# Gathering experts' rows as 16 dense tiles and copying each use within SBUF, in a two-layer mixture-of-experts and attention kernel

## Chip, cores and metric

The kernel runs on one core of a Trainium2 chip. The metric is the device time of one execution, in microseconds; before the change the median of three runs is 521.12 us (520.67 to 521.65).

## What is computed

The input x has 4 x 256 = 1024 tokens of width 256. Three blocks follow one another, each on a layer norm of x: half of a feed-forward layer is added, then attention with 16 heads of width 128, then half of the same feed-forward layer again. The feed-forward layer is what the change touches:

```python
shared = silu(g) * u @ shared_down_w.T            # g, u: 704 wide
shared = sigmoid(x @ shared_gate_w.T) * shared
probs  = softmax(x @ gate_w.T)                    # 8 experts
top_w, top_i = top_k(probs, 2); top_w /= top_w.sum()
he  = silu(x @ w1[e, :176].T) * (x @ w1[e, 176:].T)
out = sum over the 2 chosen e of top_w * (he @ w2[e].T) + shared
```

Each token goes to 2 of 8 experts, so there are 2048 pairs of token and expert.

## The kernel before

**Tiling.** Tokens are handled in NT = 8 blocks of 128. A pair gets a slot: the experts' pairs stand one after the other, and each expert's start is padded to a multiple of 128. With 2048 pairs and eight experts at most NM = 16 + 7 = 23 tiles of 128 slots are needed, each of one expert. The kernel always works through 23.

**Routing.** `route` (L731) picks the two experts, `ranks` (L1119) counts on TensorE, `slots` (L769) makes slot numbers. `rows_of_slots` (L813) writes one-hot rows (`row_hot`), `tiles_of_slots` (L800) one-hot tiles times a token number (`token_hot`, 23 columns for each of two parts). `slot_tokens` (L1131) multiplies the two in 16 small bf16 matmuls, so that for each slot its token stands in PSUM; it comes behind `shared_up(7)` in PE's order (L1163). `tokens` (L834) turns this into `place` (where a row is written back) and `tok_i` (where it is read), in four linked VectorE instructions. "Linked" means that each waits for the one before by a semaphore. `tile_experts` (L821) finds each tile's expert in three more.

**Expert tiles.** For tile m, POOL gathers 128 rows of the normed x from DRAM (`gather`, L567) into one of XR = 10 buffers; PE turns it (`tile_in`, L1140), ACT and DVE split it in a high and a low part (`tile_high` L630, `tile_low` L856), PE multiplies (`up` L1179), ACT and DVE make silu times product, PE turns this (`inner_turn` L1190) and multiplies again (`down` L1196), ACT copies the result out of PSUM (`tile_out` L686) into one of YR = 6 buffers, and POOL scatters it to DRAM (`scatter`, L575). `step` (L1211) is PE's order for three tiles in flight.

**Order on the queues.** The order on every engine is written out by hand. POOL issues gathers and scatters in one queue:

```python
for m in range(NM + OUT_LAG):        # L581, OUT_LAG = 12
    if m < NM: gather(m)
    if m >= OUT_LAG: scatter(m - OUT_LAG)
```

PE comes to the tiles from the shared expert: `first_down(1)`, then `shared_up(latest, first_tile)` (L1226, latest = 8), whose middle holds `first_tile` with `tile_in(0)`; then PE waits for `s_hl` 8, the low part of shared chunk 7 (`shared_low(7)`, L756, on DVE), ahead of `tile_in(1)` (L1227). The DVE order there is L911 to L928: `shared_mul(6)`, `tokens`, `tile_experts`, `shared_low(6)`, `gate_weights`, `lows_of("experts")`, `shared_mul(7)`, `shared_low(7)`, `shared_out(0)`, `tile_low(0)`. The weights are also split in high and low parts, in 23 jobs (`job_low`, L430) shared between POOL and DVE by the tables at L51 to L54; jobs 19 to 22 are DVE's `lows_of("experts")` in layer one.

**The end of a layer.** SP waits until all scatters have landed (L537), loads both rows of every token from DRAM (L539), and DVE adds them to x (`add`, L965, L975). In layer two the results then go out (L546).

Of the kernel before, what the change touches and what calls it, by code (L numbers as in the profile page):

```python
# [5 lines left out]
FP32 = mybir.dt.float32  # L6
FP32R = mybir.dt.float32r
BF16 = mybir.dt.bfloat16
# [5 lines left out]
P = 128  # L14
# [3 lines left out]
KD = D // P  # L18
# [11 lines left out]
STW = 3 * D  # L30
# [4 lines left out]
NM = TOP_K * NT + NE - 1  # L35
# [4 lines left out]
OUT_LAG = 12  # L40
XR = 10
YR = 6
NST = 4
# [11 lines left out]
HIGHS_FIRST = {"turn0": (1, 2), "logits0": (3, 4, 5), "silu0": (6,), "high0": (7,), "turn1": (8,), "silu2": (9, 10),  # L55
               "logits1": (11, 12), "silu3": (13, 14), "silu5": (15,), "high5": (16, 17, 18), "silu6": (19,),
               "silu7": (20, 21, 22)}
# [8 lines left out]
C_M128 = C_DESC + NE  # L66
C_LT = C_M128 + NT
# [4 lines left out]
C_VOID = C_J + TOP_K * NT  # L72
# [8 lines left out]
def constants():  # L81
# [10 lines left out]
    c[:, C_M128:C_M128 + NT] = P * np.arange(NT)  # L92
# [5 lines left out]
    c[:, C_J:C_J + TOP_K * NT] = VOID + np.arange(TOP_K * NT)  # L98
    c[:, C_VOID:C_VOID + NM] = P * np.arange(NM) + r[:, None]
# [4 lines left out]
def macaron(nc, x_in, consts, wgate, wgu, wd, w1, w2, wqkv, wo, bqkv, bo, out):  # L104
    ctx = ExitStack()
    with ctx:
# [15 lines left out]
        xn = sbuf("xn", [P, NT, D])  # L122
# [25 lines left out]
        s_xe = [sem(f"s_xe{b}") for b in range(XR)]  # L148
# [9 lines left out]
        area = sbuf("area", [P, NST * STW])  # L158
        assert QKV + (XR + YR - NT - 2) * D <= NST * STW and QKV + 2 * TOK + 2 * D <= 2 * NE * D
# [112 lines left out]
        def ffn(tag, first, n, after):  # L272
# [7 lines left out]
            with loc:  # L280
# [8 lines left out]
                tile_hot = bank[5][:, P:P + TOP_K * NT * NM].rearrange("p (a b) -> p a b", b=NM)  # L289
# [5 lines left out]
                spare = [area[:, QKV + (2 + b) * D:QKV + (3 + b) * D] for b in range(XR + YR - NT - len(lgT))]  # L295
                xe = [xn[:, b, :] for b in range(NT)] + spare[:XR - NT]
                ye = lgT + spare[XR - NT:]
                assert len(xe) == XR and len(ye) == YR
# [5 lines left out]
                token_hot = sb("token_hot", [P, TOP_K * NT, 2, NM], BF16)  # L304
                place = sb("place", [P, NM], I32)
                tok_i = sb("tok_i", [P, NM], I32)
                he = [sb(f"he{b}", [P, IM]) for b in range(2)]
# [15 lines left out]
                best = sb("best", [P, NT])  # L323
                best2 = sb("best2", [P, NT])
                lead = sb("lead", [P, NT])
# [3 lines left out]
                tiles_of = in_bank(at_tiles, [NE])  # L329
                base = sb("base", [P, NE])  # L330
# [53 lines left out]
                def ring_uses(m, depth):  # L384

                    return (0 if first else -(-(NM - m % depth) // depth)) + m // depth
# [1491 lines left out]
```

## Time and profile before

| | |
|---|---|
| median of three runs | 521.12 us |
| the profiled execution, its own time | 521.58 us |
| its span in the profile | 519.8 us |
| PE busy | 503.7 us, 97% |
| DVE busy | 348.1 us, 67% |
| POOL busy | 279.2 us, 54% |
| ACT busy | 276.0 us, 53% |
| granted TensorE clock, mean | 0.996 |

"Layer one" below is the first feed-forward layer, about 0 to 112 us of the span, "layer two" the second, about 400 to 520 us; attention lies between. The span is the time between the first and last instruction that the profile shows; the run's own time is 1.8 us longer. Rows of the timeline give the start in microseconds from the span's start, the duration, the engine, the line, what is written from what, the count, and in brackets how long the engine had been idle and what ended that.

### The profile page before, as it was taken

How to read it: one execution, taken by the hardware profiler on the slowest of the kernel's cores; microseconds unless marked ns; L12 is line 12 of the kernel's file. 1: busy time of each engine (PE TensorE's matmuls, PEld its weight loads, DVE VectorE, ACT ScalarE, POOL GpSimd, SP SyncE). 2: the span in 40 equal slices, each digit the busy share in tenths (PEclk: the TensorE clock that was granted, in tenths of full speed). 3: DMA queues.
4: the chain of work that ended last, by engine and by line, in shares of the span. 5: the costliest groups of instructions: out<-in, count | busy, mean ns of one | idle time of the engine just before them, and what ended most of it. 6: DMA issues, size and time to landing. Idle time of an engine off the chain costs nothing.

```text
span 519.8 us, 10686 instructions
## 1 busy us (share of the span) xinstructions
PE 503.7 (97%) x3329; PEld 452.5 (87%) x3329; DVE 348.1 (67%) x922; ACT 276.0 (53%) x815; POOL 279.2 (54%) x371
## 2 busy tenths in 40 slices
PE   8999999998999999999999999999999999999994
PEld 4787999887798998999988989999988788899983
DVE  5788766489464775856846847658558578866646
ACT  3983666624462654645636736546445465466540
POOL 1896777732861671652734716716542242677740
PEclk9999999999999999999999999999999999999998
DMA  8951333252002001010010010010001230233335
GB/s 274 388 191 52 105 106 106 103 164 70 21 0 62 2 22 61 20 61 0 20 61 0 20 61 15 14 52 20 0 2 42 81 123 0 83 102 106 108 123 193
DMA packets 20128, 39.41 MB, mean 76 GB/s; under 512 B 2944, under 2 KB 10496, under 8 KB 20096
## 3 DMA queue, kind: packets, MB, share of 16 engines
q1 hardware_dynamic: 15680, 26.92, 15.6%
q0 software_dynamic: 4416, 12.06, 7.1%
q8 instruction: 20, 0.33, 0.3%
q14 instruction: 12, 0.10, 0.1%
HBM read 29.80 MB, written 9.18 MB: 75 GB/s over the span
## 4 chain that ended last, share of the span: by engine, by line
PE 88%; DVE 7%; DMA 1%; issue 1%; POOL 1%; ACT 1%; SPq 0%; POOLq 0%; DVEq 0%
PE bank L183 21%; PE bank L185 20%; PE bank L184 20%; PE bank L1708 5%; PE bank L1720 4%; PE bank L1707 3%; PE bank L1749 3%; PE bank L1144 2%; DVE x_res L975 2%; PE bank L1020 2%; PE bank L189 1%; PE bank L1747 1%; PE bank L190 1%; DMA xn<-y_by_token 1%; PE bank L1192 1%
## 5 line engine op out<-in xcount | busy, mean ns | idle before, releaser
L1452 POOL TENSOR_TENSOR s_a<-s_a,rr_a 128x128 f32<-128x128 f32 x64 | 25.7, 401 | 133.6 <-DVE rr_a L1569 132.8
L1502 ACT ACTIVATE s_a<-s_a,mn_a 128x128 f32<-128x128 f32 (+1 forms) x128 | 57.1, 458 | 18.6 <-DVE mn_a L1563 18.4
L183 PE MATMUL bank<-xT_h,area_h 128*128 128x512 f32 x124 | 51.3, 414 | 0.0
L1495 ACT ACTIVATE qk_a<-bank,bias_a 128x512 f32<-128x512 f32 x32 | 22.0, 688 | 51.2 <-PE bank L185 48.5
L185 PE MATMUL bank<-xT_h,area_l 128*128 128x512 f32 x124 | 48.6, 392 | 0.0
L184 PE MATMUL bank<-xT_l,area_h 128*128 128x512 f32 x124 | 48.5, 391 | 0.0
L571 POOL DMA_INDIRECT xn<-x_normed,tok_i_f x38 | 37.2, 979 | 20.1 <-issue 9.8
L1517 ACT ACTIVATE area_h<-bank,bias_a 128x256 fp32r<-128x256 f32 x64 | 29.0, 478 | 29.3 <-PE bank L1749 28.6
L1551 DVE TENSOR_SCALAR qk_a<-bank,bias_a 128x512 f32<-128x512 f32 x32 | 24.0, 750 | 29.9 <-PE bank L185 29.9
L1563 DVE TENSOR_REDUCE mn_a<-s_a 128x1 f32<-128x128 f32 (+1 forms) x128 | 39.2, 347 | 2.2
L1559 DVE SCALAR_TENSOR_TENSOR s_a<-bank,cst 128x384 f32<-128x384 f32 x64 | 35.2, 549 | 8.1 <-PE bank L1708 8.0
L183 PE MATMUL bank<-area_h,xT_h 128*128 128x256 f32 x128 | 40.3, 315 | 0.0
L1454 POOL TENSOR_TENSOR s_a<-s_a,rr_a 128x256 f32<-128x256 f32 x64 | 39.3, 614 | 0.0
L183 PE MATMUL bank<-area_h 128*128 128x256 f32 x128 | 38.6, 301 | 0.0
L1708 PE MATMUL bank<-qk_a 128*128 128x256 f32 x128 | 38.2, 381 | 0.0
L577 POOL DMA_INDIRECT y_by_token<-rows_f,place_f x32 | 31.4, 982 | 9.7 <-issue 7.6
L185 PE MATMUL bank<-area_h,area_l 128*128 128x256 f32 x128 | 36.2, 283 | 0.0
L184 PE MATMUL bank<-area_l,area_h 128*128 128x256 f32 x128 | 36.2, 282 | 0.0
L185 PE MATMUL bank<-area_h,xT_l 128*128 128x256 f32 x128 | 36.1, 282 | 0.0
L184 PE MATMUL bank<-area_l,xT_h 128*128 128x256 f32 x128 | 36.1, 282 | 0.0
L1580 DVE SCALAR_TENSOR_TENSOR area_l<-bank,bias_a,area_h 128x256 fp32r<-128x256 f32 x64 | 30.1, 479 | 8.4 <-ACT area_h L1517 7.8
L183 PE MATMUL bank<-xT_h,wgu_h 128*128 128x512 f32 x88 | 35.4, 402 | 0.0
(210 smaller groups left out, 1712.1 us busy)
## 6 DMA issues: line engine op xcount, KB each, us to landing
area<-in_wqkv SPq DMA_DIRECT2D x8, 768.0 KB, 4.2
area_r<-in_w SPq DMA_DIRECT2D x16, 256.0 KB, 4.3
w_r<-in_w SPq DMA_DIRECT2D x8, 352.0 KB, 7.4
x_normed<-xn SPq DMA_DIRECT2D x4, 512.0 KB, 4.9
area<-in_wo SPq DMA_DIRECT2D x8, 256.0 KB, 2.6
xn<-y_by_token SPq DMA_DIRECT2D x8, 256.0 KB, 4.0
x_res<-in_x_in SPq DMA_DIRECT2D x4, 256.0 KB, 4.4
wgu_r<-in_wgu SPq DMA_DIRECT2D x4, 256.0 KB, 7.0
```

The lines of the kernel that those rows point to most:

```text
L183: pe.matmul(psum, lhs[0], rhs[0], start=first, stop=False)
L184: pe.matmul(psum, lhs[0], rhs[1], start=False, stop=False)
L185: return pe.matmul(psum, lhs[1], rhs[0], start=False, stop=last)
L571: pool.indirect_dma_start(xe[m % XR], None, xd, bass.IndirectOffsetOnAxis(ap=tok_i[:, m:m + 1], axis=0)).then_inc(s_xe[m % XR], 16)
L577: pool.indirect_dma_start(yd, bass.IndirectOffsetOnAxis(ap=place[:, m:m + 1], axis=0), ye[m % YR], None).then_inc(s_yst[m % YR], 16)
L1454: pool.tensor_tensor(s[b][:, P:3 * P], s[b][:, P:3 * P], rr[:, b, 1:2].to_broadcast([P, 2 * P]), ALU.mult).then_inc(s_p, 1)
L1502: act.activation(s[b][:, cols], s[b][:, cols], ACT.Exp, bias=mn[:, b, t:t + 1], scale=-1.0, accum_out=rs[:, b, t:t + 1]).then_inc(s_e, 1)
L1517: act.activation(zT_h[:, h, bt * SEQ:(bt + 1) * SEQ], bank[ZB[u % 2]][:, 0:SEQ], ACT.Identity, bias=bias[:, 2, h:h + 1]).then_inc(s_zh, 1)
L1559: dve.scalar_tensor_tensor(s[b][:, :], bank[3 + u % 2][:, 0:3 * P], -INV_SCALE, cst[:, C_MASK:C_MASK + 3 * P], ALU.mult, ALU.max).then_inc ...
L1563: dve.tensor_reduce(mn[:, b, t:t + 1], s[b][:, cols], op=ALU.min, axis=AX.X).then_inc(s_mn, 1)
L1580: dve.scalar_tensor_tensor(zT_l[:, h, cols], bank[ZB[u % 2]][:, 0:SEQ], bias[:, 2, h:h + 1], zT_h[:, h, cols].bitcast(FP32), ALU.add, ALU. ...
L1708: pe.matmul(b[:, P:3 * P], q[:, t0 + P:t0 + 2 * P], k[:, t0:t0 + 2 * P], start=True, stop=True).then_inc(s_sc, 1)
```

## The change

The 2048 pairs are laid out with no padding, as NX = 16 dense tiles. A dense tile can hold rows of more than one expert. There are still 23 uses ("items"): one for each tile and expert that meet, and one more for unused ones. POOL gathers only the 16 dense tiles, into XR = 12 buffers. For each item but the first SP reads from `tile_x` which buffer holds its tile and copies it within SBUF (128 KB) into one of XI = 4 buffers `xi`, from which PE turns it; item 0 is turned straight from buffer 0. Rows of a tile that belong to another expert get a place in a void part of DRAM. Copy m waits for gather m (m below 16; gathers of buffers 8 and 9 share a semaphore, as do 10 and 11) and for `tile_in(m - 4)`. Gathers 12 to 15 wait for copies 7 to 10. The result buffers fall from 6 to 4.

POOL issues gathers 0 to 3, in layer one then the low parts of weight jobs 20 to 22, then gathers 4 to 11, then scatters 0 to 3, then gathers 12 to 15 by turns with scatters 4 to 6, then the other scatters. Job 19 goes to POOL too, ahead of the gathers; ACT makes the high parts of jobs 19 to 22 behind `shared_silu(6)`.

On DVE `slots` has two linked instructions fewer, `tokens` is one instruction, `items_of_experts` adds six small ones ahead of it, and `tile_experts` has ten in place of three. `items_of_slots` adds three and a second set of one-hots 23 columns wide; `places` has three and waits for a second set of 16 matmuls on PE, `item_tokens`. `slot_tokens` becomes 32 matmuls of 16 columns, and moves to the middle of `shared_up(7)`. The norms are as they were. The core of the diff:

```diff
+NX = TOP_K * NT
+NM = NX + NE - 1
...
-XR = 10
-YR = 6
-NST = 4
+XR = 12
+YR = 4
+XI = 4
...
-POOL_FIRST = {"rstd0": (2,), "normed": (3, 5, 6, 7, 8, 9, 10, 11, 12, 13, 14, 15, 16, 17, 18)}
+POOL_FIRST = {"rstd0": (2,), "normed": (3, 5, 6, 7, 8, 9, 10, 11, 12, 13, 14, 15, 16, 17, 18, 19), "gathers": (20, 21, 22)}
...
-LOWS_FIRST = {"stats1": (1,), "xn1": (4,), "experts": (19, 20, 21, 22)}
+LOWS_FIRST = {"stats1": (1,), "xn1": (4,)}
...
+                    x_at = sp.alloc_register(f"x_at_{tag}")
+                    sp.wait_ge(s_expert, 2)
+                    for m in range(1, NM):
+                        sp.reg_load(x_at, tile_x[0:1, m:m + 1])
+                        if m == 1:
+                            sp.wait_ge(s_xe[0], 16 * (ring_uses(0, XR, NX) + 1))
+                        if m < NX:
+                            sp.wait_ge(s_xe[gathered(m)], (32 if m % XR >= NT else 16) * (ring_uses(m, XR, NX) + 1))
+                        if m > XI:
+                            sp.wait_ge(s_tx, m - XI + 1)
+                        sp.dma_start(xi[:, m % XI, :], xe[:, sp.snap(x_at, min_val=0, max_val=XR - 1), :]
+                                     ).then_inc(s_xi[m % XI], 16)
...
-                    def gather(m):
-                        if m >= XR:
-                            pool.wait_ge(s_tx, m - XR + 1)
+                    def gather(t):
+                        if t >= XR:
+                            m = t - XR + NE - 1
+                            pool.wait_ge(s_xi[m % XI], 16 * (copies_before(m) + 1))
+                            pool.wait_ge(s_tx, 1)
                         pool.indirect_dma_start(
-                            xe[m % XR], None, xd,
-                            bass.IndirectOffsetOnAxis(ap=tok_i[:, m:m + 1], axis=0)).then_inc(s_xe[m % XR], 16)
+                            xe[:, t % XR, :], None, xd,
+                            bass.IndirectOffsetOnAxis(ap=tok_i[:, t:t + 1], axis=0)).then_inc(s_xe[gathered(t)], 16)
...
-                    for m in range(NM + OUT_LAG):
-                        if m < NM:
-                            gather(m)
-                        if m >= OUT_LAG:
-                            scatter(m - OUT_LAG)
+                    for t in range(XR):
+                        gather(t)
+                        if t == 3:
+                            lows_of("gathers")
+                    pool.wait_ge(s_tok, 2)
+                    for m in range(NM):
+                        scatter(m)
+                        if XR <= XR + m - 3 < NX:
+                            gather(XR + m - 3)
...
+                    def hot(tile, into, n, blocks):
+                        copies = [P, TOP_K * NT, n]
+                        part = tile_hot[:, 0:TOP_K * NT * n].rearrange("p (a b) -> p a b", b=n)
+                        link(dve.tensor_tensor(part, tile[:, :].unsqueeze(2).to_broadcast(copies),
+                                               cst[:, C_MP:C_MP + n].unsqueeze(1).to_broadcast(copies),
+                                               ALU.is_equal))
+                        dve.tensor_scalar(into[:, :, 0, :], part, cst[:, C_P:C_P + 1], None,
+                                          ALU.mult).then_inc(s_hot, 1)
...
+                        hot(slot_tile, token_hot_x, NX, C_T)
...
+                    def items_of_experts():
+                        link(dve.tensor_copy(start_i[:, :], base[:, :]))
...
+                    def items_of_slots():
+                        link(dve.tensor_tensor(chosen, sel[:, :, :, :].rearrange("p t a b -> p (t a) b"),
+                                               extra[:, :].unsqueeze(1).to_broadcast([P, TOP_K * NT, NE]), ALU.mult))
+                        link(dve.tensor_reduce(slot_item[:, :], chosen, op=ALU.add, axis=AX.X))
+                        link(dve.scalar_tensor_tensor(slot_item[:, :], slot_item[:, :], float(P), slot_tile[:, :],
+                                                      ALU.mult, ALU.add))
+                        hot(slot_item, token_hot, NM, C_J)
...
+                        dve.tensor_copy(tok_i[:, :], bank[5][:, 0:NX]).then_inc(s_tok, 1)
...
+                    def places():
+                        dve.wait_ge(s_inv, 2)
+                        code = bank[5][:, ITEMS + NM:ITEMS + 2 * NM]
                         link(dve.scalar_tensor_tensor(tok_f, code, 0.0, cst[:, C_VOID:C_VOID + NM],
                                                       ALU.is_equal, ALU.mult))
-                        link(dve.tensor_tensor(tok_f, bank[5][:, 0:NM], tok_f, ALU.add))
-                        link(dve.scalar_tensor_tensor(place[:, :], code, float(P), tok_f, ALU.mult, ALU.add))
-                        dve.tensor_scalar(tok_i[:, :], place[:, :], TOK - 1, None,
-                                          ALU.bitwise_and).then_inc(s_tok, 1)
+                        link(dve.tensor_tensor(tok_f, bank[5][:, ITEMS:ITEMS + NM], tok_f, ALU.add))
+                        dve.scalar_tensor_tensor(place[:, :], code, float(P), tok_f, ALU.mult,
+                                                 ALU.add).then_inc(s_tok, 1)
...
                     tiles_of_slots()
                     shared_mul(6)
+                    items_of_experts()
                     tokens()
                     tile_experts()
                     shared_low(6)
+                    items_of_slots()
+                    shared_mul(7)
+                    places()
                     gate_weights()
-                    lows_of("experts")
-                    shared_mul(7)
...
-                            last = pe.matmul(bank[5][:, 0:2 * NM], row_hot[:, q, :],
+                            for a in range(2):
+                                last = pe.matmul(bank[5][:, 0:NX], row_hot[:, q, :], token_hot_x[:, q, a, :],
+                                                 start=q + a == 0, stop=q + a == TOP_K * NT)
+                        last.then_inc(s_inv, 1)
+                    def item_tokens():
+                        pe.wait_ge(s_hot, 5)
+                        for q in range(TOP_K * NT):
+                            last = pe.matmul(bank[5][:, ITEMS:ITEMS + 2 * NM], row_hot[:, q, :],
                                              token_hot[:, q, :, :].rearrange("p a b -> p (a b)"),
                                              start=q == 0, stop=q == TOP_K * NT - 1)
                         last.then_inc(s_inv, 1)
-                    def tile_in(r, b):
-                        pe.wait_ge(s_xe[r % XR], 16 * (ring_uses(r, XR) + 1))
+                    def tile_in(m, b):
+                        if m == 0:
+                            pe.wait_ge(s_xe[0], 16 * (ring_uses(0, XR, NX) + 1))
+                        else:
+                            pe.wait_ge(s_xi[m % XI], 16 * (copies_before(m) + 1))
+                        rows_in = xi[:, m % XI, :] if m else xe[:, 0, :]
                         for k in range(KD):
                             last = pe.transpose(bank[pair_x + b][:, k * P:(k + 1) * P],
-                                                xe[r % XR][:, k * P:(k + 1) * P], ident)
+                                                rows_in[:, k * P:(k + 1) * P], ident)
...
-                    shared_up(7)
-                    slot_tokens()
+                    shared_up(7, slot_tokens)
...
                     def first_tile():
+                        item_tokens()
                         pe.wait_ge(s_silu, latest)
                         tile_in(0, 0)
-                        pe.wait_ge(s_expert, 1)
+                        pe.wait_ge(s_expert, 2)
```

## Rows read from the trace of the kernel before

**Rows 1.** The page: the span, busy time by engine, and the group of gathers.
```profile
span 519.8 us, 10686 instructions
...
PE 503.7 (97%) x3329; PEld 452.5 (87%) x3329; DVE 348.1 (67%) x922; ACT 276.0 (53%) x815; POOL 279.2 (54%) x371
...
L571 POOL DMA_INDIRECT xn<-x_normed,tok_i_f x38 | 37.2, 979 | 20.1 <-issue 9.8
```

**Rows 2.** Waits in the stretch 480 to 500 us: total us, times, longest.
```profile
ACT rows_f L691 <- DMA y_by_token<-rows_f,place_f: 1.7, 2, 1.1
...
ACT area L691 <- DMA y_by_token<-area,place_f: 1.4, 1, 1.4
```

**Rows 3.** Timeline of PE, layer one: start us, us, line, operation, count.
```profile
41.51 0.57 PE L1135 MATMUL bank<-token_hot_f,rows_f 128*128 128x46 bf16 x16
...
46.08 0.40 PE L183 MATMUL bank<-xT_h,wgu_h 128*128 128x512 f32 x1
...
47.48 0.38 PE L1144 MATMUL bank<-cst,xn 128*128 128x128 f32 x2
...
55.86 0.38 PE L1144 MATMUL bank<-cst,xn 128*128 128x128 f32 x2
...
78.11 0.38 PE L1144 MATMUL bank<-cst,xn 128*128 128x128 f32 x2
...
92.52 0.38 PE L1144 MATMUL bank<-cst,xn 128*128 128x128 f32 x2
```

**Rows 4.** Timeline of PE, layer two.
```profile
445.61 0.40 PE L183 MATMUL bank<-xT_h,wgu_h 128*128 128x512 f32 x1
...
454.01 0.38 PE L1144 MATMUL bank<-cst,xn 128*128 128x128 f32 x2
...
491.18 0.38 PE L1144 MATMUL bank<-cst,xn 128*128 128x128 f32 x2
```

**Rows 5.** Timeline of DVE, layer one.
```profile
38.79 0.54 DVE L804 TENSOR_TENSOR bank<-bank,cst 128x368 f32<-128x368 int32 x1
...
42.12 0.18 DVE L841 SCALAR_TENSOR_TENSOR sel_f<-bank,cst 128x23 f32<-128x23 f32 x1 [1.10 <-PE bank L1135]
...
42.34 0.18 DVE L843 TENSOR_TENSOR sel_f<-bank,sel_f 128x23 f32<-128x23 f32 x1
...
44.23 0.15 DVE L851 TENSOR_SCALAR gates_r_f<-gates_f 128x16 f32<-128x16 f32 x1
...
45.20 2.55 DVE L434 TENSOR_TENSOR area_l<-area_r,area_h 128x512 fp32r<-128x512 f32 x4
...
49.02 0.69 DVE L761 TENSOR_TENSOR hT_l_f<-bank,hT_h_f 128x512 fp32r<-128x512 f32 x1 [0.66 <-ACT hT_h_f L628]
```

**Rows 6.** Timeline of DVE, layer two.
```profile
446.00 0.69 DVE L761 TENSOR_TENSOR hT_l_f<-bank,hT_h_f 128x512 fp32r<-128x512 f32 x1 [0.66 <-ACT hT_h_f L628]
...
509.06 0.48 DVE L975 SCALAR_TENSOR_TENSOR x_res<-xn,gates_r_f,x_res 128x256 f32<-128x256 f32 x1 [0.74 <-DMA xn<-y_by_token]
...
509.93 0.48 DVE L975 SCALAR_TENSOR_TENSOR x_res<-xn,gates_r_f,x_res 128x256 f32<-128x256 f32 x1 [0.39 <-DMA xn<-y_by_token]
```

**Rows 7.** Timeline of POOL, both layers.
```profile
36.11 5.06 POOL L434 TENSOR_TENSOR area_l<-area_r,area_h 128x512 fp32r<-128x512 f32 x4
...
43.82 1.17 POOL L571 DMA_INDIRECT xn<-x_normed,tok_i_f  x1 [2.64 <-DVE tok_i_f L845]
...
500.73 0.97 POOL L577 DMA_INDIRECT y_by_token<-area,place_f  x1 [0.30 <-issue]
```

**Rows 8.** The gathers' own line L571: from issue to landing.
```profile
DMA to landing us min/median/max: 2.7/2.7/3.0
```

**Rows 9.** The scatters' own line L577: from issue to landing.
```profile
DMA to landing us min/median/max: 2.4/2.4/3.8
```

**Rows 10.** The output stores L546, 128 KB each from SBUF: issue to landing.
```profile
DMA to landing us min/median/max: 1.8/2.6/4.2
```

**Rows 11.** Timeline of ACT at the end of layer two.
```profile
498.42 0.39 ACT L691 ACTIVATE area<-bank 128x256 f32<-128x256 f32 x1 [0.46 <-PE bank L190]
```

More of the change, by code:

```diff
@@ L147, in macaron @@
         y_before = [0] * NT
-        s_xe = [sem(f"s_xe{b}") for b in range(XR)]
+        s_xe = [sem(f"s_xe{b}") for b in range(NT + (XR - NT) // 2)]
+        s_xi = [sem(f"s_xi{b}") for b in range(XI)]
         s_yst = [sem(f"s_yst{b}") for b in range(YR)]
@@ L157, in macaron @@
         QKV = 3 * KD * 2 * DH
[L158 to L159 removed]
+        SPARE = XR - NT
+        area = sbuf("area", [P, QKV + 2 * D + XR * D])
+        assert QKV + 2 * TOK + 2 * D <= 2 * NE * D and SPARE >= 4
+        xe = area[:, QKV + 2 * D:].rearrange("p (b d) -> p b d", d=D)
+        xn = xe[:, SPARE:, :]
         w_raw, wo_raw = area[:, 0:QKV], area[:, QKV:QKV + 2 * D]
@@ L294, in ffn @@
                 lgT = [rows[:, a, :] for a in range(4)]
[L295 to L298, printed above, removed]
+                ye = lgT
+                assert len(ye) == YR
                 xeT_h = [sb(f"xeT_h{b}", [P, KD * P], FP32R) for b in range(2)]
@@ L303, in ffn @@
                 assert row_hot.shape[1] == TOK // P * TOP_K
-                token_hot = sb("token_hot", [P, TOP_K * NT, 2, NM], BF16)
+                hot_room = sb("hot_room", [P, TOP_K * NT * 2 * NM], BF16)
+                token_hot = hot_room[:, :].rearrange("p (a b c) -> p a b c", b=2, c=NM)
+                token_hot_x = hot_room[:, 0:TOP_K * NT * 2 * NX].rearrange("p (a b c) -> p a b c", b=2, c=NX)
+                xi = sb("xi", [P, XI, D])
                 place = sb("place", [P, NM], I32)
-                tok_i = sb("tok_i", [P, NM], I32)
-                he = [sb(f"he{b}", [P, IM]) for b in range(2)]
+                tok_i = sb("tok_i", [P, NX], I32)
+                he_both = hot_room[:, :].bitcast(FP32)
+                he = [he_both[:, b * IM:(b + 1) * IM] for b in range(2)]
                 heT_h = [sb(f"heT_h{b}", [P, 2 * P], FP32R) for b in range(2)]
@@ L322, in ffn @@
                 assigned = sb("assigned", [P, NT + 1, NE], BF16)
-                best = sb("best", [P, NT])
+                best, lead, base, extra, slot_item = [
+                    wg_tile[:, NM * (NE + 1) + a * NE:NM * (NE + 1) + (a + 1 if a < 4 else 6) * NE] for a in range(5)]
+                assert NT == NE and NM * (NE + 1) + 6 * NE <= KD * P
                 best2 = sb("best2", [P, NT])
-                lead = sb("lead", [P, NT])
                 own = sb("own", [P, NT])
@@ L381, in ffn, with ring_uses, gathered, copies_before @@
                 s_out = None if first else sem("s_out")
-                def ring_uses(m, depth):
-                    return (0 if first else -(-(NM - m % depth) // depth)) + m // depth
+                def ring_uses(m, depth, count):
+                    return (0 if first else -(-(count - m % depth) // depth)) + m // depth
+                def gathered(t):
+                    b = t % XR
+                    return b if b < NT else NT + (b - NT) // 2
+                def copies_before(m):
+                    per_layer = len(range(m % XI or XI, NM, XI))
+                    return (0 if first else per_layer) + len(range(m % XI or XI, m, XI))
                 jobs = []
@@ L798, in slots @@
                         dve.tensor_scalar(slot_row[:, :], slot_i[:, :], P - 1, None, ALU.bitwise_and).then_inc(s_slot, 1)
+                    def hot(tile, into, n, blocks):
[6 more added lines that the diff above has]
+                                          ALU.mult).then_inc(s_hot, 1)
+                        dve.tensor_tensor(into[:, :, 1, :], part,
+                                          cst[:, blocks:blocks + TOP_K * NT].unsqueeze(2).to_broadcast(copies),
+                                          ALU.mult).then_inc(s_hot, 1)
```

92 lines of the change are left out of this document (48 added, 44 removed).

## The prediction

> **What bounds the kernel now.** I read the page first, then the waits of the second layer's end, then PE's timeline where the shared expert hands over to the expert tiles, then DVE's and POOL's beside it. PE is busy for 503.7 of 519.8 us and all else for at most 67% [rows 1]. So a gain has to come out of the 16 us in which PE is idle, and whatever puts a new wait on PE costs its full length. POOL pays 0.98 us for a gather and 0.30 us (9.8 us of issue over 32 of them) until the next [rows 1], so 1.28 us an indirect DMA; a gather and a scatter for each tile take 2.56 us, while PE needs 2.02 us a tile (11 steps between 55.86 and 78.11) [rows 3]. POOL therefore falls behind, in spite of its head start, and shows it late: 3.1 us of waits of ACT for a result buffer whose scatter hasn't landed, three in all [rows 2], and a last scatter at 500.73 [rows 7] whose rows were ready at 498.42 + 0.39 = 498.81 [rows 11]. That backlog is all there is to win.
>
> **What it can win.** In layer two the 18 steps from tile 4 to tile 22 take 491.18 - 454.01 = 37.2 us [rows 4]; at 2.02 each they would take 36.4, so 0.8 us. The same steps in layer one: 92.52 - 55.86 = 36.7 [rows 3], so 0.3 us. At the very end DVE waits 0.74 and 0.39 us for the rows that come back from DRAM [rows 6], together 1.1 us. Seven gathers fewer are 7 x 1.28 = 9 us of POOL in a layer, more than the backlog, so all three go if nothing new comes. Layer one's additions show no such wait. Most: 0.3 + 0.8 + 1.1 = 2.2 us.
>
> **PE's own part.** 16 small matmuls take (0.57 - 0.18) / 15 = 26 ns apart, 0.41 us in all [rows 3] (0.18 us is the length of one). Now there are 32 of 16 columns ahead of the tiles, and 16 more of 46. If the cost went by columns the 32 would cost 32 x 9 ns = 0.3 us; if by instruction, 0.8. Each has its own load of 128 x 128 weights, which doesn't shrink, so I take 26 ns: +0.4 us for the first set, 0.4 for the second, in each layer. The Trainium skill (TensorE: Matmul & The Clock Gate, section "Wait — 56ns, not 53.3ns?") has a floor of about 25 ns from start to start however few the columns. By that rule the set costs 0.8 us, as I took it; by columns alone the forecast would be about 1 us lower over both layers.
>
> **The hand-over, where I expect the loss.** DVE's `shared_low(7)` must be done before PE may turn tile 1. It now stands behind `places`, and `places` behind `item_tokens`, which is in the middle of `shared_up(8)`. Layer one: `shared_up(8)` starts at 46.08 [rows 3], now 46.49; its first half takes 47.48 - 46.08 = 1.40, so `item_tokens` starts at 47.89. From the first small matmul to DVE's first use was 42.12 - 41.51 = 0.61 [rows 3, 5], so `places` starts at 48.50. Its three instructions are 0.22 apart [rows 5]: 0.65. `gate_weights` takes 45.20 - 44.23 = 0.97 [rows 5]. `shared_low(7)` starts at 50.1 in place of 49.02 [rows 5]: +1.1 us. In layer two it is 445.61 [rows 4] + 0.41 + 1.40 + 0.61 + 0.65 + 0.97 = 449.65 in place of 446.00 [rows 6]: +3.6 us. There it had slack: tile 4 came 8.0 us after it, and in layer one, where it bound, 6.8 us (454.01 - 446.00, 55.86 - 49.02). So 1.2 us are covered and 2.4 us reach PE.
>
> The other DVE edits I cost at nothing. Before this point DVE loses two linked steps of 0.26 us and a third of the width of three one-hot instructions (0.54 us for 368 elements [rows 5]), and gains six small ones ahead of `tok_i`, three off it, so the first gather is held by POOL, not by DVE, in layer one. Seven more in `tile_experts` (estimated at 0.25 each, a little over the 0.22 of the small rows) and `items_of_slots` (three at 0.25, three one-hots at 0.54: 2.4 us) end near 47.3 in layer one. What hides them is that `places` can't start before 48.5; with this cover gone (PE earlier by 1.2 us) each would count in full.
>
> **The gathers and the copies.** A gather lands 2.7 us after its issue [rows 8]. For a copy of 128 KB within SBUF there is no row; the nearest is the output store, 128 KB out of SBUF by the same queue, 1.8 to 4.2 us with a median of 2.6 [rows 10]. I take 2.6, and both ends for the range, with 0.15 us for SP to notice. Another 22 DMAs on SP are behind all loads of weights and ahead of the loads at L539, which wait for the last scatter anyway; XI = 4 gives each three steps, 6 us, to land. The Trainium skill (SBUF — State Buffer, "The DMA setup-cost knee") charges every DMA some 2 us whatever its size, plus bytes at 436 GB/s: 2.3 us here. By it the rule speaks against the change, 22 more of these fixed costs a layer, but the sum would be only 0.3 us lower.
>
> Layer one: POOL's last job ends at 41.17, job 19 adds 5.06 / 4 = 1.27 [rows 7], and gather 0 starts near 42.75 (43.82 before). Gather 3 starts at 46.8, then three jobs of 1.27, and gather 4 starts at 51.9 and lands at 54.6; the copy lands at 57.4. PE wants tile 4 at 55.86 + 1.1 = 56.95: 0.4 us late. From gather 4 to gather 15 there are 18 indirect DMAs of 1.28, as scatters 0 to 6 are now among them: gather 15 starts at 74.9, its copy lands at 80.4, and PE wants it at 78.11 + 1.1 + 0.4 = 79.6: 0.8 us late. Layer two has no jobs there and no wait: gather 15 starts by about 472.3 (it is behind scatter 6, whose rows are ready when tile 10 has been turned, 454.0 + 2.4 + 6 x 2.02 + 0.6 = 469.1, and behind the pairs ahead of it), its copy lands at 477.7, and PE wants it at 454.0 + 2.4 + 11 x 2.02 = 478.6.
>
> YR = 4: a scatter lands in 2.4 to 3.8 us [rows 9] and a buffer comes round in 4 x 2.02 = 8.1. It costs nothing as long as POOL is less than 4 us behind. In layer one scatter 0 starts near 62.2 and lands at 64.6, ACT wants its buffer when tile 8 has been turned, near 65.6, so this cover is 1.1 us thin.
>
> **The sum.** Layer one: 1.1 + 0.4 + 0.8 - 0.3 = +2.0 us. Layer two: +2.4 - 0.8 = +1.6 us on PE, less 1.1 us of DMA waits at the end (the last scatter starts near 501.0, against 500.73, while DVE comes 1.6 us later): +0.5. Together +2.5 us. Against the profiled run's own 521.58 this is 524.1; the median is 0.46 lower, so **523.6 us**. By the bounds of the copy: 1.8 us takes both late tiles of layer one down to 0.4 in all, the sum 1.7; 4.2 us makes the tiles of layer one 2.8 late in all beyond the 1.1 and adds 0.7 in layer two, the sum 4.8.
>
> **The rivals.** *Faster: the hand-over and POOL's order are both covered.* It decides at two places: the copy for tile 15 of layer one would have to be there by 78.1, 2.3 us before I expect it, and `shared_low(7)` of layer two be late by no more than its slack of 1.2 us and the 0.4 us of `slot_tokens`. Then layer one gives -0.3 and layer two 0.4 - 0.8 - 1.1 = -1.5, in all -1.8: 519.3 us. For it speaks that the first indices come over 1 us earlier and that all my times on POOL rest on one spacing of 1.28; against it that the orders of DVE and POOL are fixed in the code and both places are late by sums of several rows. 10%. *No difference.* Half of the delay in layer two is hidden and the copies take 1.8 us, so that the 2.2 us won pay for nearly all: 1.7 - 1.2 = +0.5, 521.6. 22%. *Copies slow.* The register read, the wait and the copy take 4.2 us or more: +4.8, 525.9 us. 18%. *The change doesn't relieve POOL,* since 23 scatters stay and gathers 12 to 15 sit among them: then none of the 2.2 us is won and the rest is paid, 4.7 us, 525.8; this lies in the forecast's range, and I count it there. My forecast has 50%.
>
> **The numbers.** About 0.2% (1.04 us) is what a measurement can tell from no change, 520.1 to 522.2. Slower by more: the forecast and the slow copies, 0.68. Within: 0.22. Faster: 0.10. The range runs from 520.3, which leaves out the faster rival, to 526.3, with the long copies in.
>
> **What would show it.** In the changed profile: 32 gathers at L571's successor in place of 46; `shared_low(7)` at about 50.1 and 449.6; tile 1 turned right behind it; in layer one a wait of PE for a copy at tiles 4 and 15; no wait of ACT for a scatter after the first four; a step of 2.02 us to the end; no wait of DVE for y rows in layer two. I am wrong if `places` runs before `shared_up(8)` is half done, if a copy takes outside 1.8 to 4.2 us, or if the steps of tiles grow beyond 2.02 us.

## The result and the profile after

The changed kernel takes **526.01 us** (median of 4 runs, 525.41 to 526.14); the kernel before takes 521.13 beside it (4 runs, 520.67 to 521.65). The ratio is **1.0084, 95% interval [1.0071, 1.0097]**: slower by about 4.4 us. (The two medians lie 4.9 us apart; what follows uses the ratios, and the spans of the two profiles, which are 4.4 us apart.) The profiled execution took 525.96 us itself, with a span of 524.2. I had forecast 523.6 with a range of 520.3 to 526.3, and slower with 0.68. The direction was right and the time lies inside the range, at its upper end. The size, +2.5 us, was too small, and nearly all of what was missing lies in one place.

The page of the kernel after: span, busy time by engine, the groups of gathers and scatters.

```profile
span 524.2 us, 11005 instructions
...
PE 507.3 (97%) x3393; PEld 455.1 (87%) x3393; DVE 355.9 (68%) x952; ACT 277.1 (53%) x815; POOL 269.9 (51%) x361
...
L611 POOL DMA_INDIRECT y_by_token<-rows_f,place_f x46 | 44.8, 973 | 36.3 <-ACT rows_f L729 32.4
...
L605 POOL DMA_INDIRECT area<-x_normed,tok_i_f x32 | 30.9, 967 | 14.3 <-issue 8.5
```

Against [rows 1]: 32 gathers in two layers, and POOL is 9.3 us less busy. POOL's idle time now ends on ACT's rows (32.4 us, 33 times): the scatters wait for the results, not the results for the scatters as in [rows 2]. So the change does what it set out to do. The loss is elsewhere, and PE's timeline of layer one finds it.

Timeline of PE after, layer one: start us, us, line, operation, count, and the idle time before it.

```profile
47.46 0.57 PE L1220 MATMUL bank<-hot_room_f,rows_f 128*128 128x46 bf16 x16
47.88 0.42 PE L1233 MATMUL bank<-cst,area 128*128 128x128 f32 x2
...
52.36 0.44 PE L1233 MATMUL bank<-cst,xi_f 128*128 128x128 f32 x2 [1.97 <-DVE hT_l_f L799]
...
53.58 0.49 PE L185 MATMUL bank<-w_l,xeT_h_f 128*128 x1
53.87 0.49 PE L186 MATMUL bank<-w_h,xeT_l_f 128*128 x1
...
60.14 0.38 PE L1233 MATMUL bank<-cst,xi_f 128*128 128x128 f32 x2
...
96.83 0.38 PE L1233 MATMUL bank<-cst,xi_f 128*128 128x128 f32 x2
```

L1233 is `tile_in`: tiles 0, 1, 4 and 22. Tile 4 comes at 60.14 where it came at 55.86 [rows 3], 4.3 us late; tile 22 at 96.83 against 92.52, still 4.3. Nothing is lost or won in the 18 steps between: 36.69 us here, 36.66 before, so the 0.3 us that I had hoped to win in them did not come. No tile waits for its copy. All of it happens before tile 4: PE idles 1.97 us for `shared_low(7)`, and then it is slow, with matmuls that start 0.29 us apart where they start 0.16 apart before and later. DVE's timeline shows what it waited for.

Timeline of DVE after, layer one.

```profile
48.07 0.18 DVE L916 SCALAR_TENSOR_TENSOR sel_f<-bank,cst 128x23 f32<-128x23 f32 x1 [0.77 <-PE bank L1220]
...
48.60 2.28 DVE L925 TENSOR_SCALAR gates_r_f<-gates_f 128x16 f32<-128x16 f32 x1
50.92 0.25 DVE L926 RECIPROCAL gates_r_f<-gates_r_f 128x16 f32<-128x16 f32 x1
...
51.62 0.69 DVE L799 TENSOR_TENSOR hT_l_f<-bank,hT_h_f 128x512 fp32r<-128x512 f32 x1
```

Timeline of POOL after, layer one: gather 3, the low parts of weight jobs 20 to 22, gather 4.

```profile
46.10 0.95 POOL L605 DMA_INDIRECT area<-x_normed,tok_i_f  x1 [0.30 <-issue]
47.08 3.76 POOL L454 TENSOR_TENSOR area_l<-area_r,area_h 128x512 fp32r<-128x512 f32 x3
51.00 0.97 POOL L605 DMA_INDIRECT area<-x_normed,tok_i_f  x1 [0.16 <-issue]
```

L925 is the first instruction of `gate_weights`, 16 numbers in each partition. It took 0.15 us before [rows 5]; now it takes 2.28, and it ends at 50.88, right as POOL's three subtractions end at 47.08 + 3.76 = 50.84.

The stretch behind it, of after: us, busy us and count of each engine, granted clock, DMA share, GB/s.

```profile
50.00:53.00 3.00, 0.83 (x4) 0.20 (x2) 2.86 (x8) 0.16 (x1) 2.54 (x3) 1.00 0.24 70
53.00:56.00 3.00, 2.69 (x10) 2.63 (x11) 2.08 (x6) 0.83 (x3) 2.11 (x3) 0.59 0.44 122
56.00:59.00 3.00, 3.00 (x18) 2.72 (x18) 2.03 (x6) 1.74 (x7) 2.37 (x3) 0.84 0.69 198
59.00:62.00 3.00, 2.71 (x17) 2.27 (x18) 1.99 (x6) 1.20 (x6) 1.89 (x3) 1.00 0.63 180
```

PE was busy for 0.83 of the 3 us from 50 to 53, and then the granted clock is a mean of 0.59 and 0.84 in place of 1.00: part of that time at the lower level, 1.2 GHz. (Taken microsecond by microsecond it is 0.77, 0.50, 0.50 and 0.52 from 53 to 57, and 1.00 on either side.) From tile 1 to tile 4 PE takes 60.14 - 52.36 = 7.8 us, against 55.86 - 49.76 = 6.1 before. The same windows of the kernel before all show 1.00, and its share of the DMA engines from 56 to 59 is 0.39 where it is now 0.69.

Layer two, timeline of DVE after.

```profile
452.32 0.18 DVE L916 SCALAR_TENSOR_TENSOR sel_f<-bank,cst 128x23 f32<-128x23 f32 x1 [0.77 <-PE bank L1220]
...
452.86 0.16 DVE L925 TENSOR_SCALAR gates_r_f<-gates_f 128x16 f32<-128x16 f32 x1
...
453.77 0.69 DVE L799 TENSOR_TENSOR hT_l_f<-bank,hT_h_f 128x512 fp32r<-128x512 f32 x1
...
515.50 0.48 DVE L1051 SCALAR_TENSOR_TENSOR x_res<-area,gates_r_f,x_res 128x256 f32<-128x256 f32 x1 [0.22 <-DMA area<-y_by_token]
```

There POOL has no subtractions, and L925 takes its 0.16 us. Tile 4 of layer two is turned at 460.92 and tile 22 at 497.69, 6.9 and 6.5 us behind [rows 4]; with the 4.3 brought along (PE's first product of `wg_h`, where this layer begins, starts at 416.00 in place of 411.71) that is +2.6 and then 0.4 back. At the end DVE waits 0.22 us for rows where it waited 0.74 + 0.39 [rows 6].

### The profile page after: what moved, and what is told of

Same layout as the page of the kernel before. It is cut to its first block, busy times and chain, and to the rows that moved or that the text cites. A ratio compares the mean times of both kernels' runs of the same rounds, so it can differ in the third digit from the quotient of the medians.

```text
span 524.2 us, 11005 instructions
## 1 busy us (share of the span) xinstructions
PE 507.3 (97%) x3393; PEld 455.1 (87%) x3393; DVE 355.9 (68%) x952; ACT 277.1 (53%) x815; POOL 269.9 (51%) x361
## 4 chain that ended last, share of the span: by engine, by line
PE 89%; DVE 7%; DMA 1%; issue 1%; POOL 1%; ACT 1%; SPq 0%; DVEq 0%; POOLq 0%
PE bank L184 21%; PE bank L185 20%; PE bank L186 20%; PE bank L1797 5%; PE bank L1809 4%; PE bank L1796 3%; PE bank L1838 3%; PE bank L1233 2%; DVE x_res L1051 2%; PE bank L190 2%; PE bank L1096 1%; PE bank L191 1%; PE bank L1836 1%; PE bank L1280 1%; DMA area<-y_by_token 1%
## 5 line engine op out<-in xcount | busy, mean ns | idle before, releaser
L611 POOL DMA_INDIRECT y_by_token<-rows_f,place_f x46 | 44.8, 973 | 36.3 <-ACT rows_f L729 32.4
L605 POOL DMA_INDIRECT area<-x_normed,tok_i_f x32 | 30.9, 967 | 14.3 <-issue 8.5
```

The lines of the kernel that those rows point to most:

```text
L605: pool.indirect_dma_start(xe[:, t % XR, :], None, xd, bass.IndirectOffsetOnAxis(ap=tok_i[:, t:t + 1], axis=0)).then_inc(s_xe[gathered(t)], 16)
L611: pool.indirect_dma_start(yd, bass.IndirectOffsetOnAxis(ap=place[:, m:m + 1], axis=0), ye[m % YR], None).then_inc(s_yst[m % YR], 16)
```

## The experiments

The theory: in layer one `gate_weights` is held by POOL's subtractions, and PE's gap then costs clock. Its rivals: DVE's order alone is too long, the copies and their traffic are what costs, or the seven gathers fewer were never worth anything. Times are medians beside runs of the kernel before on the same chip.

**The changed kernel once more**, for a second profile.

> The changed kernel as it is, on the chip of the three runs that follow, so that they have their own base. 1.0084 times the kernel before, within its interval, for every theory.

Measured: 526.3 us, 521.69 before, ratio 1.0093 [1.0068, 1.0118]. In its profile L925 took 2.27 us from 49.24 on and PE idled 1.9 us, but the clock stayed at 1.00 in the windows behind it, and tile 4 came 6.6 us after tile 1 in place of 7.8. So the held instruction comes in both profiles and the clock's fall in one of them, where it costs about 1.2 us. The mean granted clocks of the single executions point the same way: of these six, three with 0.996 to 0.998 took 523.8 to 525.6 us, and three with 0.992 or 0.993 took 527.0 to 528.1; the four of the first measurement all had 0.994 and took 525.4 to 526.1. That is a difference of more than 1.2 us, and what else differs between those executions is not shown.

**The gate weights through PSUM.** The same arithmetic with PSUM as destination, and one copy more; the product behind it reads PSUM too.

```diff
-link(dve.tensor_scalar(gates_r[:, :, :], gates[:, :, :], 1.0, None, ALU.add))
-link(dve.reciprocal(gates_r[:, :, :], gates_r[:, :, :]))
-link(dve.tensor_scalar(gates_r[:, :, :], gates_r[:, :, :], 0.5, None, ALU.mult))
+link(dve.tensor_scalar(gates_p, gates[:, :, :], 1.0, None, ALU.add))
+link(dve.reciprocal(gates_p, gates_p))
+link(dve.tensor_scalar(gates_p, gates_p, 0.5, None, ALU.mult))
+link(dve.tensor_copy(gates_r[:, :, :], gates_p))
...
```

> The changed kernel, but the four small gate_weights instructions of DVE go through PSUM (one more, a copy back), so that none of them reads and writes SBUF alone. Port theory: in the changed kernel the first of them took 2.28 us in place of 0.15, since POOL's three subtractions hold what the two engines share in SBUF until 50.84; that made PE idle 2.0 us and then run at the lower clock, 3.8 us in all. Then here the row is 0.2 us long, PE keeps its clock, tile 4 of layer one is turned about 3.5 us earlier, and the time is about 522.5 us. Rival, the order alone (places behind the small matmuls in the middle of shared_up(8)): the long row is only where that wait shows, and the time stays at 526.0, or 0.2 above for the added instruction.

Timeline of DVE in this run: the first instruction of `gate_weights` and `shared_low(7)`, here L927 and L801.

```profile
49.04 0.17 DVE L927 TENSOR_SCALAR bank<-gates_f 128x16 f32<-128x16 f32 x1
...
50.16 0.69 DVE L801 TENSOR_TENSOR hT_l_f<-bank,hT_h_f 128x512 fp32r<-128x512 f32 x1
```

Measured: 525.17 us, 1.0058 [1.0045, 1.007]. POOL subtracts just the same beside it, and the instruction takes 0.17 us: with its result in PSUM it is not held. `shared_low(7)` is at 50.16, where I had predicted 50.1, and tile 4 at 57.35 in place of 60.14, 2.8 us earlier. But of the 3.5 us that I expected only 1.4 came back in the time, and the trace shows two places where some of it is lost again. With PE earlier, steps of 2.3 and 2.45 us in place of 2.0 appear at tiles 7 and 12 (the copy of tile 12 took 4.84 us), and the 18 steps take 94.95 - 57.35 = 37.6. And at the end of layer two, which PE's tile 22 reaches 2.2 us before the changed kernel's, DVE waits 1.7 us for the rows that come back from DRAM, where it waited 0.22: the last scatter took 4.58 us to land and not 2.41. Why it did is not known; so the gain of this run rests on the trace more than on its time.

**PE kept busy in the gap**: 18 idle matmuls ahead of tile 1, in layer one.

```diff
 shared_up(latest, first_tile)
+if first:
+    keep_warm(pe, 4, 18)
```

> The changed kernel with 18 idle matmuls of 256 columns (bf16, about 0.11 us apart, 2.0 us) on PE in layer one between shared_up(8) and the wait ahead of tile 1, into a bank that nothing uses there. The DVE stall stays. Clock theory: the matmuls after the gap no longer run at the lower clock (0.29 us apart for the expert's up products, 0.16 before), and 1.7 us come back: 524.3 us. Rival: the slow matmuls behind the gap come from what feeds them, not from the clock: 526.0, or a little above if the added ones delay tile 1.

Measured: 525.37 us, 1.0070 [1.0055, 1.0086]. The first two of the four windows, as above, are now

```profile
50.00:53.00 3.00, 2.73 (x22) 1.88 (x20) 2.86 (x8) 0.23 (x1) 2.54 (x3) 1.00 0.26 81
53.00:56.00 3.00, 2.79 (x19) 2.65 (x19) 2.78 (x7) 0.97 (x4) 2.09 (x4) 1.00 0.45 138
```

and the clock is 1.00 in all four. DVE's L925 still took 2.22 us, tile 1 came at 52.29 as before, and tile 4 at 58.75 in place of 60.14. In the trace the clock is worth these 1.4 us. In the times the interval overlaps that of the changed kernel, so there it is not shown on its own.

**The subtractions behind gather 5** in place of gather 3.

```diff
-if t == 3:
+if t == 5:
     lows_of("gathers")
```

> The changed kernel with POOL's three subtractions (jobs 20 to 22) behind gather 5 in place of gather 3, so that they start near 49.6 and no longer when DVE comes to gate_weights (48.6). Same work, nothing else moved. Port theory: the DVE row is back at 0.15 us, PE's gap is under 1 us and its clock stays up: 3 us or more come back, about 1.0025 times the kernel before. Rival, that the long row belongs to the instruction or to what it reads: unchanged, 1.0084.

Measured: 528.47 us, 1.0128 [1.0109, 1.0147], slower still, against the expectation. Timeline of DVE in this run:

```profile
48.45 0.18 DVE L925 TENSOR_SCALAR gates_r_f<-gates_f 128x16 f32<-128x16 f32 x1
...
48.95 4.20 DVE L927 TENSOR_SCALAR gates_r_f<-gates_r_f 128x16 f32<-128x16 f32 x1
```

and of POOL:

```profile
48.42 0.95 POOL L605 DMA_INDIRECT area<-x_normed,tok_i_f  x1 [0.30 <-issue]
49.39 3.71 POOL L454 TENSOR_TENSOR area_l<-area_r,area_h 128x512 fp32r<-128x512 f32 x3
```

The first instruction gets by, since the subtractions now begin later; gather 5, whose issue began at 48.42, did not hold it. The third, the next one from SBUF to SBUF, starts while gather 5 is being issued and ends at 53.15, right behind the last subtraction at 49.39 + 3.71 = 53.10. It was held 4 us, over the rest of a gather and three subtractions, without getting in between: on POOL they follow one another within 0.02 us. My expectation had counted only which instruction lay beside the subtractions as the order stood, not that the next one would run into them. PE's gap was 3.9 us, the granted clock of the 3 us from 56 on was 0.51, and tile 4 came at 61.74, 1.6 us after the changed kernel's. This run is the strongest evidence for the theory: the delay moves with the subtractions and grows with the time for which they hold. Its time is longer by more than that. Of the 3.1 us between the two spans, 1.3 are left at tile 22 of layer two, and the rest comes at the end, where DVE waits 1.8 us for rows behind a last scatter that took 4.14 us to land.

The Trainium skill has this rule (SBUF — State Buffer, section "Who interferes with whom"): VectorE and GpSimd share one pair of SBUF ports, an exclusive lock; `tensor_scalar` can enter the two-port modes that take it, on certain conditions, while an instruction with at most one SBUF input outside those modes does not contend. The runs agree as to which instructions are held: `tensor_scalar` from SBUF to SBUF in two places, and not the first of them with its result in PSUM (0.17 us). The page speaks of the length of one instruction; here it was a run of several.

**The gate weights early**, ahead of `shared_low(6)`, where POOL issues gathers.

```diff
 tile_experts()
+gate_weights()
 shared_low(6)
 items_of_slots()
 shared_mul(7)
 places()
-gate_weights()
```

> The changed kernel with gate_weights ahead of shared_low(6) in place of behind places, in both layers. Port theory: it runs before POOL's three subtractions start, so the 3.8 us of layer one go, and besides 0.97 us leave the path to shared_low(7) in both layers, of which PE can use about 0.3 in layer one and 0.8 in layer two: about 521.2 us, unless PE, now early, has to wait for copies (tile 15 of layer one, up to 0.7 us): 521.9. Rival, the order alone: only the 0.97 us twice, 524.2 us.

Measured: 522.65 us, **1.0007 [0.9997, 1.0017]**. Moving four small instructions takes back 4.0 us of the change's 4.4 (by the ratios). `shared_low(7)` is at 49.92, tile 1 at 51.45, tile 4 at 56.90. That is more than the hold and the clock alone, since the four instructions, 0.97 us, also leave the path to `shared_low(7)` in both layers. What stays over the kernel before lies in the 18 steps of layer one, which take 95.19 - 56.90 = 38.3 us: 0.75 is a wait for the copy of tile 6, and the steps from tile 6 to tile 13 are 2.05 to 2.17 long. The chain of waits for tile 6 (start us, us, what):

```profile
54.27 3.29 DMA area<-x_normed,tok_i_f
...
57.69 4.35 DMA xi_f<-area
...
62.08 0.44 PE bank L1233 x2
```

The gather is number 6. It took 3.3 us to land where [rows 8] had 2.7, and the copy behind it 4.35, above the 4.2 with which I had bounded it. In the changed kernel itself PE came too late to meet it. In this run too an instruction from SBUF to SBUF beside a gather seems to have been held, a little: L927 took 0.43 us and ended at 45.31, at the same moment as gather 1 (44.36 + 0.95).

**The kernel before with 16 gathers.** Gathers 16 to 22 of each layer are left out, and PE turns what the buffers hold, so the last seven tiles of a layer have rows of other tiles. Its result is not the kernel's; it only prices the gathers.

```diff
-if m < NM:
+if m < TOP_K * NT:
     gather(m)
```

> The kernel before, with gathers 16 to 22 of both layers left out and their tiles turned from whatever the buffer holds, so part of the experts' input is old rows. Nothing else is changed, and nothing is copied. It prices POOL's relief alone. By my sum 0.3 us in layer one and 0.8 + 1.1 us in layer two: 518.9 us, no wait of ACT for a scatter, no wait of DVE for rows at the end. Rival, the backlog is hidden: 521.1 us as before.

Measured: 519.81 us, **0.9961 [0.9948, 0.9974]**, so 2.0 us. The gain that I had put at 2.2 us at most is real, and the rest of the change costs more than it. In its trace the 18 steps of layer two take 490.41 - 454.03 = 36.4 us and DVE waits for no rows at the end; in layer one they take 36.6, so the 0.3 us that I had put there is hardly seen.

**Gate weights early, without the copies.** PE turns the gathered buffers directly; 22 copies a layer are left out, and so tiles past the boundaries of experts hold rows of other tiles. This too is only a price.

```diff
-sp.dma_start(xi[:, m % XI, :], xe[:, sp.snap(x_at, min_val=0, max_val=XR - 1), :]
-             ).then_inc(s_xi[m % XI], 16)
...
-rows_in = xi[:, m % XI, :] if m else xe[:, 0, :]
+rows_in = xe[:, min(m, NX - 1) % XR, :]
```

> gate_weights early and the 22 copies a layer left out: tile m is turned from the buffer of gather m, or of the last gather from tile 16 on, so parts of the experts' input are rows of other tiles. It prices the copies in that order. If they cost PE only the wait at tile 6 and a little elsewhere, about 1.2 us come back against the run with gate_weights early: 0.9985 times the kernel before. If copies cost nothing: 1.0007. Gathers should land in 2.7 to 2.8 us again.

Measured: 520.48 us, 0.9978 [0.9969, 0.9988]. Against the same order with copies (1.0007) the copies cost 0.29% or 1.5 us, and it is lost in layer one: the 18 steps take 93.24 - 56.51 = 36.7 us in place of 38.3. Without copies the gathers from 50 to 62 us landed in a median of 2.7 us again.

**Both: gate weights early and the subtractions behind gather 5.**

```diff
-if t == 3:
+if t == 5:
     lows_of("gathers")
...
 tile_experts()
+gate_weights()
 shared_low(6)
```

> gate_weights early and the three subtractions behind gather 5, both. If what is left over the kernel before in the run with gate_weights early (1.0007) is the wait of PE for the copy of tile 6 (its gather took 3.3 us and its copy 4.4 us while both streams ran together), then with gathers 4 and 5 3.8 us earlier that wait of about 1 us goes: 0.999 times the kernel before. If the DMA engines' load is what makes copies slow wherever they stand, another tile waits and it stays at 1.0007.

Measured: 522.55 us, 1.0017 [1.0007, 1.0026]. Neither of the two outcomes that I had named, 0.999 and 1.0007. No wait at tile 6 any more, but tiles 15 and 16 of layer one come in steps of 2.5 and 2.4 us, and the 18 steps from tile 4 to tile 22 take 94.02 - 56.33 = 37.7 us. Gather 15 was issued at 74.11 and took 3.02 us to land, its copy 2.23. This is the second late copy of my prediction (74.9 there, 0.8 us of lateness): it exists, and it shows once PE is early enough to meet it.

**Gathers 12 to 15 sooner.** Four runs moved these in POOL's queue, all with the gate weights early; the first three by two scatters, of which the first two have the subtractions behind gather 5 and the third has them behind gather 3.

```diff
-if XR <= XR + m - 3 < NX:
-    gather(XR + m - 3)
+if XR <= XR + m - 1 < NX:
+    gather(XR + m - 1)
```

> As the run with the gate weights early and the subtractions behind gather 5 (1.0017), with one thing more: gathers 12 to 15 are issued behind scatters 1 to 4 in place of 3 to 6. In that run gather 15 was issued at 74.1 us and tile 15 was turned at 79.5, one and a half microseconds after the pace of 2.0 a tile would have had it, so the 18 steps from tile 4 to tile 22 took 37.7 us where before had 36.7. Two scatters earlier is about 4 us earlier. If the last gathers are what is late: the 18 steps are 36.7 to 36.9 us again, and the ratio 0.9998 (1.0017 less 0.9 us of 521.5). If the copies themselves are late, being slow at a DMA share of 0.7: steps over 2.1 us stay at other tiles, and the ratio stays at 1.0015.

Measured: 521.84 us, 1.0002 [0.9991, 1.0013]. The time is the one expected, but not for the reason expected: the 18 steps took 94.29 - 56.24 = 38.05 us. The wait has changed places. Timeline of ACT in this run:

```profile
72.66 0.39 ACT L729 ACTIVATE rows_f<-bank 128x256 f32<-128x256 f32 x1 [2.09 <-DMA y_by_token<-rows_f,place_f]
```

Four gathers between scatters 1 to 4 put the scatters off, and ACT waited for one of the YR = 4 result buffers; PE lost 1.04 us behind it. The prediction had called this cover "1.1 us thin".

> As the last run, and the scatters' places (three small DVE instructions, about 0.6 us) are moved behind the low half of tile 0, so that they are no longer ahead of the hand-over to the first tiles. If DVE's order ahead of the hand-over still costs its length, tile 1 is turned 0.5 us earlier in layer one, in layer two tile 4 as well, and the ratio is 0.9985 to 0.999. If the copies set the pace once TensorE is early, as when the gate weights alone were sped up, tile 4 comes no earlier and the ratio is that of the last run.

```diff
 shared_out(0)
 tile_low(0, 0)
+places()
 shared_out(1)
```

(`places` is taken out ahead of the hand-over.) Measured: 522.52 us, 1.0008 [0.9997, 1.0018]. DVE's order is 0.6 us shorter ahead of the hand-over, and tile 1 came at 50.92, against 50.78 in the run before it: no gain. `shared_low(7)` now waits 0.7 us for ACT's high part, and PE waits 0.4 us for a low half on DVE and 0.43 for the copy of tile 6. From here on DVE's order is not what sets tile 1.

> Gate weights early and gathers 12 to 15 behind scatters 1 to 4, the subtractions left behind gather 3. With the gate weights alone early the ratio was 1.0007, with a wait of 0.75 us for the copy of tile 6 (its gather lies behind the subtractions) and no wait at tile 15. If the last gathers matter only where the subtractions lie late, this gives 1.0007 again; if they delay others too, by taking POOL's time ahead of the scatters, 1.001 or more.

Measured: 522.67 us, 1.0014 [1.0002, 1.0026]. The subtractions behind gather 3 make tile 4 wait 0.58 us for its copy, as the prediction had it (0.4). That copy took 2.97 us.

**One sooner instead of two**: behind scatters 2 to 5, the subtractions behind gather 5, the gate weights early.

```diff
-if XR <= XR + m - 1 < NX:
-    gather(XR + m - 1)
+if XR <= XR + m - 2 < NX:
+    gather(XR + m - 2)
```

> Gate weights early, the subtractions behind gather 5, and gathers 12 to 15 behind scatters 2 to 5: halfway between the run with them behind scatters 3 to 6 (1.0017; tiles 15 and 16 of layer one 0.5 and 0.4 us late) and the one behind scatters 1 to 4 (1.0002; ScalarE waited 2.09 us for a scatter in layer one, and TensorE 1.04 us for it). If the two costs are ends of one queue on POOL, with room between them: neither wait, 18 steps of layer one in 37.0 us or less, ratio 0.999, which would be the first version below the kernel before. If there is no room between: one of the waits stays, at half its size, and the ratio is 1.000 to 1.001.

Measured: 520.99 us, **0.9988 [0.9979, 0.9997]**. The 18 steps take 93.56 - 56.73 = 36.8 us in layer one and 493.45 - 456.86 = 36.6 in layer two, and neither ACT nor PE waits for a scatter or a copy there. It is the only version with the kernel's own result that lies below the kernel before, by 0.6 us, and it is the last of six orders with the gate weights early.

## Why the prediction was right, and where it was not

**What bounds it, and what can be won: right.** The backlog of POOL is gone, and seven gathers fewer are worth 2.0 us on their own, 2.2 predicted. In the changed kernel the 0.3 us of layer one did not show (36.69 us against 36.66).

**The small matmuls: right.** 32 of 16 columns took 0.97 us in layer two, (0.97 - 0.18) / 31 = 25.5 ns apart, 26 predicted. It goes by the instruction, not by the columns.

**Layer two's hand-over: right.** `shared_low(7)` was predicted at 449.65; it came at 453.77, of which 4.3 was brought along from layer one, so 3.5 us late of its own where 3.6 was predicted. Of its lateness 2.4 us should reach PE, and 2.6 did. The steps gave back 0.4 of 0.8, DVE's waits at the end 0.9 of 1.1. The stores of the results then landed faster, 2.0 us in the median against 2.6 [rows 10], which may be some of the 1.2 us by which the time from the start of DVE's last work to the end is shorter (4.5 before, 3.3 after). Layer two as a whole stands at +0.1 us, +0.5 predicted.

**Layer one's hand-over: the step that failed.** "`gate_weights` takes 45.20 - 44.23 = 0.97" carried a duration from a place where POOL had no subtractions beside it to one where it had. It took 3.0 us, 2.28 of them for its first instruction. `shared_low(7)` came at 51.62 instead of 50.1: +2.6 us where I had +1.1. Without the 2.1 us it would have come 0.6 early, since `shared_up(8)` began at 46.07 and not 0.4 later as I worked out. "The other DVE edits I cost at nothing" passed over the same thing: the diff takes the subtractions from DVE, where they cannot collide with its own instructions, and gives them to POOL. I had priced what POOL does with them (the late gather 4) and not what they do to DVE. A gap of 2 us on PE then brought another 1.2 us at the lower clock in the profiled execution, a term that I did not have. 2.6 and 1.2 are 3.8 of the 4.3 us at tile 4. The rest is not settled: from tile 1 to tile 4 PE took 6.4 to 6.6 us at full clock as well, where it took 6.1 before. Most of that lies between tile 3 and tile 4 (2.9 us against 2.6); in both profiles of the changed kernel and in the run with the idle matmuls PE stops there for 0.3 to 0.5 us ahead of the last two matmuls of tile 0's `down`, and the profile names nothing that ends the stop.

That the time still fell inside the range is partly luck. For layer one I had 1.1 + 0.4 + 0.8 - 0.3 = +2.0; the trace has 2.6 + 1.2 + 0.5 = +4.3, with no copy waited for and nothing won in the steps. The upper end of the range stood there for slow copies, and the held instruction and the clock filled its place.

**The late copies: right in mechanism, hidden in fact.** Tiles 4 and 15 did not wait in the changed kernel, where PE was 2.6 to 4.3 us late already. In the runs with PE early both waits appeared, 0.58 us at tile 4 and 0.5 at tile 15. The copy's own time, taken as 2.6 with 1.8 and 4.2 as bounds, was 2.23 and 2.97 us on the chains of tiles 15 and 4, but 4.35 and 4.84 at tile 6 and tile 12 of two other runs, above the upper bound.

**The rivals.** "Faster" needed `shared_low(7)` and the copy of tile 15 both in time; neither was. "No difference" was right for another kernel, the one with the gate weights early. "Copies slow" gives nearly the measured time, 525.9, by a cause that the trace excludes: PE waited for no copy in either layer.

**The sum, as the runs have it**: -2.0 for the gathers left out, +1.5 for the copies, +4.0 for the place of the gate weights, and the 1.6 I had for the small matmuls, which no run took alone, make +5.1 against 4.4 measured. The parts overlap, so they need not add up; the 4.0 above all holds more than the hold and the clock, as said at that run.

## What to carry to other kernels

When a change moves elementwise work from VectorE to GpSimd, look at what VectorE does in that stretch: a `tensor_scalar` of 16 numbers a partition, from SBUF to SBUF, stood still here until GpSimd's run of work ended. Take a duration from a place with the same neighbours, and where none exists bound it by the neighbour's whole run. When one late thing is repaired, the next ones in the queue appear; here three were left (the copy of tile 4 or 6, the copy of tile 15, a result buffer), and one order of POOL's queue met all three, for 0.6 us in the end.

## What was not expected of the hardware

- A VectorE `tensor_scalar` over 16 numbers a partition, fp32 from SBUF to SBUF, took 2.28, 2.22 and 2.27 us beside GpSimd's three subtractions and 4.20 us when it started ahead of them, against 0.15 to 0.20 elsewhere. With its result in PSUM it took 0.17 beside the same subtractions. The reciprocal on the same operands never lay beside them. Beside the issue of a gather the same kind of instruction took 0.18 and 0.20 us at its start, and 0.26 and 0.43 where it ended together with it.
- TensorE's granted clock fell to means of 0.59 and 0.84 over 3 us each after a gap of about 2 us in one profile (0.50 from 54 to 56 us), stayed at 1.00 after a gap of 1.9 us in another of the same kernel, and fell to 0.51 after one of 3.9 us. What decides between the first two was not found.
- Gathers land later beside copies: from 50 to 62 us of layer one in a median of 2.7 us without copies and of 3.3 with them (3.5 at most; in layer two 4.5 at most). A copy of 128 KB took from 2.23 to 4.84 us on the chains that show one.
- A scatter mostly lands in 2.4 us, but the last one of layer two took 4.58 and 4.14 us in two runs, and the end of the kernel came later by it. No run shows why.
